# A layer-norm, causal-attention and expert-FFN layer on one core: the eight steps ahead of the attention written out, with the first batch's stacks read back during them

## The reference

```
xn   = (x - mean(x)) / sqrt(var(x) + 1e-5)                    # per row
# attention branch: 16 heads of 8 channels
Q, K, V = relu(xn @ Wq + bq), relu(xn @ Wk + bk), relu(xn @ Wv + bv)
scores  = Q K^T / sqrt(8); NEG where the key's row sums to 0; NEG above the diagonal
attn    = softmax(scores), set to 0 where the query's row sums to 0
s       = gamma * norm(attn V + xn) + beta
# FFN branch
x_attn  = norm2(xn) @ attn_w.T + attn_b + xn
eo      = gelu(x_attn @ w1[e] + b1[e]) @ w2[e] + b2[e]        # expert e fixed by position
f       = gelu(eo @ next_w.T + next_b)
out     = x + s * silu(f)
```

## Time and profile before

| | |
|---|---|
| median of 3 runs | 537.47 us (536.09 to 538.89) |
| profiled execution, its own time | 538.71 us |
| span of the profile, first to last instruction | 536.9 us |
| PE busy | 447.4 us (83%) |
| DVE busy | 406.4 us (76%) |
| ACT busy | 315.3 us (59%) |
| POOL busy | 124.7 us (23%) |
| mean granted TensorE clock | 0.942 |
| DMA packets, bytes | 28585, 39.68 MB |

### The profile page before, as it was taken

The page is one execution under the profiler, slowest core; times in us unless marked ns, Lnnn a source line. Parts: engine busy times, 40 slices in busy tenths (PEclk is TensorE's granted clock), DMA queues, the critical chain, the costliest instruction groups (busy, mean ns, idle before and its releaser), DMA issues.

```text
span 536.9 us, 10757 instructions
## 1 busy us (share of the span) xinstructions
PE 447.4 (83%) x3773; PEld 275.3 (51%) x3773; DVE 406.4 (76%) x1008; ACT 315.3 (59%) x670; POOL 124.7 (23%) x345
## 2 busy tenths in 40 slices
PE   0049545988999739999999999999999999999981
PEld 0026334766777515565555555555556556556540
DVE  6898988887884238576977877877878878887715
ACT  0029135977888803566656666656667567566670
POOL 8000000000000011001045045045054063072181
PEclk9999958989999955799999999999999999999997
DMA  8900021223333351122122222322212213212000
GB/s 220 295 20 0 20 80 43 75 80 98 98 98 88 110 146 22 47 76 62 56 83 67 72 67 66 85 56 66 85 53 77 82 46 93 64 48 69 2 21 20
DMA packets 28585, 39.68 MB, mean 74 GB/s; under 512 B 5751, under 2 KB 19959, under 8 KB 28535
## 3 DMA queue, kind: packets, MB, share of 16 engines
q1 hardware_dynamic: 28486, 39.03, 26.0%
q10 hardware_dynamic: 48, 0.01, 0.0%
HBM read 25.91 MB, written 10.49 MB: 68 GB/s over the span
## 4 chain that ended last, share of the span: by engine, by line
PE 55%; DVE 6%; issue 1%; ACT 1%; DVEq 0%; ACTq 0%
PE banks L979 15%; PE banks L1010 14%; PE banks L998 13%; PE banks L981 6%; PE banks L1000 5%; DVE mx L837 3%; PE banks L1020 3%; DVE stats L879 1%; DVE aggr L883 1%; ACT pt L950 0%; ACT ots L934 0%; PE banks L988 0%; DVE res L866 0%; DVE res L869 0%; DVE mixed L870 0%
## 5 line engine op out<-in xcount | busy, mean ns | idle before, releaser
L837 DVE TENSOR_REDUCE mx<-banks 128x1 f32<-128x384 f32 (+3 forms) x384 | 212.5, 598 | 59.7 <-PE banks L981 52.5
L950 ACT ACTIVATE pt<-banks 128x512 f32<-128x512 f32 (+2 forms) x384 | 184.8, 528 | 110.4 <-PE banks L1000 104.1
L981 PE MATMUL banks<-causal,ident_b 128*128 128x128 bf16 x512 | 106.8, 228 | 0.0
L1000 PE MATMUL banks<-causalT,ident_b 128*128 128x128 bf16 x512 | 103.7, 222 | 0.0
L979 PE MATMUL banks<-w_room 73*128 73x512 bf16 (+3 forms) x256 | 75.3, 331 | 11.5 <-DVEq L912 10.3
L1010 PE MATMUL banks<-pt,vg 128*9 128x512 f32 (+3 forms) x1024 | 81.9, 438 | 0.5 <-ACT pt L950 0.5
L998 PE MATMUL banks<-w_room 76*128 76x512 bf16 (+3 forms) x256 | 71.2, 310 | 0.0
L979 PE MATMUL banks<-k_odd,q_odd 73*128 73x512 bf16 (+3 forms) x256 | 69.0, 302 | 1.6 <-DVE mx L837 1.6
L998 PE MATMUL banks<-q_odd,k_odd 76*128 76x512 bf16 (+3 forms) x256 | 67.6, 300 | 2.0 <-ACT pt L950 2.0
L750 POOL TENSOR_SCALAR mneg<-mx 128x16 f32<-128x16 f32 x32 | 8.1, 253 | 197.9 <-DVEq L845 197.9
L981 PEld LDWEIGHTS banks<-causal,ident_b 128*128 128x128 bf16 x512 | 52.1, 102 | 0.0
(11 more groups left out here) (155 smaller groups left out, 615.7 us busy)
## 6 DMA issues: line engine op xcount, KB each, us to landing
k_scratch<-parts SPq DMA_DIRECT2D x40, 128.0 KB, 2.3
w_room<-q_scratch SPq DMA_DIRECT2D x48, 96.0 KB
w_room<-k_scratch SPq DMA_DIRECT2D x48, 96.0 KB
q_odd<-q_scratch SPq DMA_DIRECT2D x48, 96.0 KB
k_odd<-k_scratch SPq DMA_DIRECT2D x48, 96.0 KB
q_scratch<-parts SPq DMA_DIRECT2D x24, 128.0 KB, 2.3
w_room<-in_w_dram SPq DMA_DIRECT2D x1, 2048.0 KB, 9.2
xn_all<-xn_st SPq DMA_DIRECT2D x8, 256.0 KB, 2.4
```

Of the source, the lines that this page charges most:

```text
L837: ins = dve.tensor_reduce(mx[:, u % 2, heads[0]:heads[-1] + 1, q], banks[:, S0 + c % RING, 0:w * len(heads)].rearrange("p (h k) -> p h k", ...
L950: act.activation(weights(k, heads[0], len(heads)), banks[:, ST0 + j % RING, 0:(T - P * k) * len(heads)], ACT.Exp, scale=SCALE).then_inc(ex ...
L981: ins = mm(o[:, w - P:w], ident_b[:, :], causal[:, :], start=False, stop=True)
L1000: ins = mm(o[:, 0:P], ident_b[:, :], causalT[:, :], start=False, stop=True)
```

## The change

1. The hardware loops of SP, ACT and PE in the first block are gone. Their eight steps are written out.
2. The buffers `cen` and `work` of the first block are now the memory of `xn_all` and `gate_all`. `quotients` writes the normalised rows straight into `xn_all`, in place. The staging buffer `xn_st`, its DMA on SP and the semaphores `keep_ready`, `xn_kept`, `norm_free` and `w1_done` are gone.
3. Batch 0's stacks have a pair of their own (`q_own`, `k_own`), and the weights' rooms serve the odd batches. SP issues the ones after step 1's stores, and the query and key stacks of groups 0 to 3 after the stores of steps 2 to 5 (6 DMAs each). The second block's loads of groups 2 and 3 and of the odd ones ahead of its loop are gone.
4. The mask is made in the last step: DVE computes `live_all` and `mask_b` before `gate` and `lows`, PE transposes between the two expert products, ACT copies it in the place of the second norm. The store to `mask_scratch` is now on SP's queue after the last K stores. SP waits for it, reads the four mask rows, then reads the odd ones, and then waits for the last Q and K stores.
5. The last step no longer makes the second norm, the transposes and the attention-weight product of a step that doesn't exist.

```diff
-    qx, kx = [stack_of(w1_room)], [stack_of(w2_room)]
+    q_own, k_own = sb("q_own", [P, E * HID]), sb("k_own", [P, E * HID])
+    qx, kx = [stack_of(q_own), stack_of(w1_room)], [stack_of(k_own), stack_of(w2_room)]
...
-        cen = s1("cen", [P, NT, C])
-        work = s1("work", [P, NT, C])
+        cen, work = xn_all, gate_all
...
             def _(sp):
...
-                with sp.Fori(0, MB) as m:
-                    tok = Tokens(sp)
-                    for n in range(STEPS):
-                        sp.wait_ge(keep_ready, tok.next(keep_ready))
-                        sp.dma_start(xn_all[:, bass.ds(m * MT + TB * n, TB), :], xn_st[:, n]).then_inc(xn_kept[n], 16)
-                        for o in range(2):
-                            sp.wait_ge(low_ready, tok.next(low_ready))
-                            for k in range(COPIES[o]):
-                                dst = (q_dram, k_dram)[o][bass.ds(m * STEPS + n, 1), k].rearrange("b d h t -> (b h) d t")
-                                sp.dma_start(dst, parts[:, o, k % PARTS, :]).then_inc(parts_out[o], 16)
-                    tok.settle()
-
-
-                sp.wait_ge(w1_done, MB * STEPS)
-                load_queries(sp, 0, 0, 0)
-                load_queries(sp, 0, 0, 1)
-                sp.wait_ge(w2_done, MB * STEPS)
-                load_keys(sp, 0, 0, 0)
-                load_ones(sp, 0)
-                load_keys(sp, 0, 0, 1)
+                tok = Tokens(sp)
+                for i in range(B):
+                    for o in range(2):
+                        sp.wait_ge(low_ready, tok.next(low_ready))
+                        for k in range(COPIES[o]):
+                            dst = (q_dram, k_dram)[o][i:i + 1, k].rearrange("b d h t -> (b h) d t")
+                            sp.dma_start(dst, parts[:, o, k % PARTS, :]).then_inc(parts_out[o], 16)
+                    if i == 1:
+                        load_ones(sp, 0)
+                    if 2 <= i < 2 + NG:
+                        load_queries(sp, 0, 0, i - 2)
+                        load_keys(sp, 0, 0, i - 2)
+                sp.wait_ge(maskT_ready, 1)
+                sp.dma_start(mask_dram, maskT[:, :]).then_inc(mask_out, 16)
                 sp.wait_ge(mask_out, 16)
-                load_mask(sp, 0, 0, 0)
-                load_mask(sp, 0, 0, 1)
+                for g in range(NG):
+                    load_mask(sp, 0, 0, g)
+                sp.wait_ge(w2_done, B)
+                load_ones(sp, 1)
+                for o in range(2):
+                    sp.wait_ge(parts_out[o], 16 * COPIES[o] * (B + 1))
...
-                def quotients(m, n):
-
-                    tiles = slice(m * MT + TB * n, m * MT + TB * n + TB)
+                def quotients(i):
+
+                    tiles = slice(TB * i, TB * i + TB)
...
-                    if m > 0:
-
-                        dve.wait_ge(norm_free, n + 1)
-                        dve.wait_ge(xn_kept[n], 16)
...
-                            (wu, nr, quo, ALU.add, xn_st[:, n])):
+                            (wu, nr, quo, ALU.add, xn_all[:, tiles, :])):
...
                     dve.sem_inc(xn_ready, 1)
-                    dve.sem_inc(keep_ready, 1)
...
-                for i in range(2, MB * STEPS):
-                    quotients(i // STEPS, i % STEPS)
+                for i in range(2, B):
+                    quotients(i)
                     rests(tok)
                     if i == 2:
                         second_roots(GROUPS[1])
-                    sums(i // STEPS, i % STEPS)
+                    sums(i)
+                    if i == B - 1:
+                        link(dve.tensor_scalar(live_all[:, :], zero_all[:, :], -1.0, 1.0, ALU.mult, ALU.add))
+                        dve.tensor_scalar(mask_b[:, :], zero_all[:, :], -BIG, None, ALU.mult).then_inc(mask_ready, 1)
                     gate(tok, i - 2)
                     lows(tok)
...
-                def gelu_out(tok):
+                def gelu_out(tok, last):
...
-                    product_out(tok)
+                    if not last:
+                        product_out(tok)
...
-                with act.Fori(0, MB) as m:
...
-                        second_norm(tok, (n + 1) % STEPS)
...
+                for i in range(B):
...
+                    if last:
+                        act.wait_ge(maskT_done, 1)
+                        act.activation(maskT[:, :], banks[:, TRX, :].bitcast(BF16)[0:NT, 0:P],
+                                       ACT.Copy).then_inc(maskT_ready, 1)
+                    else:
+                        second_norm(tok, i + 1)
...
-                act.wait_ge(maskT_ready, 1)
-                act.dma_start(mask_dram, maskT[:, :]).then_inc(mask_out, 16)
...
+                    if i == B - 1:
+                        pe.wait_ge(mask_ready, 1)
+                        pe.transpose(banks[:, TRX, :].bitcast(BF16)[0:NT, 0:P], mask_b[:, :],
+                                     ident_b[:, :]).then_inc(maskT_done, 1)
...
+                    if i < B - 1:
+                        second_normed(tok, i + 1)
+                        normed(tok, i + 1)
+                    next_product()
+                    if i < B - 1:
+                        attn_product(tok, i + 1)
...
-                for o in range(2):
-                    sp.wait_ge(parts_out[o], 16 * COPIES[o])
-                for g in range(2, NG):
-                    load(0, 0, g)
-                load_ones(sp, 1)
                 tok = Tokens(sp)
                 maxima(tok, 0, 0)
```

More of the change, by code:

```diff
@@ L211, in build_program @@
         xn_ready, sums_ready = sem("xn_ready"), sem("sums_ready")
-        xl_ready, xn_kept = sem("xl_ready"), [sem(f"xn_kept{n}") for n in range(STEPS)]
-        keep_ready = sem("keep_ready")
-        norm_free = sem("norm_free")
+        xl_ready = sem("xl_ready")
         trx_done, trl_done = sem("trx_done"), sem("trl_done")
@@ L542, in _ @@
[L542 to L546 removed]
+                for i in range(B):
+                    n, last = i % STEPS, i == B - 1
+                    for o, bias, done in ((0, bq, q_done), (1, bk, k_done)):
+                        act.wait_ge(done, tok.next(done))
+                        act.wait_ge(parts_out[o], tok.next(parts_out[o], 16 * COPIES[o]))
+                        act.activation(full[:, o, :], banks[:, QB + o, :], ACT.Relu, bias=bias)
+                        act.activation(parts[:, o, 0, :], banks[:, QB + o, :], ACT.Relu,
+                                       bias=bias).then_inc(split_ready, 1)
+                    act.wait_ge(v_done, tok.next(v_done))
+                    at = slice(TB * i, TB * i + TB)
+                    act.activation(v_all[:, at, :].rearrange("p n (h w) -> p n h w", w=VW)[:, :, :, 0:DH],
+                                   banks[:, VB, :].rearrange("p (n h d) -> p n h d", n=TB, d=DH),
+                                   ACT.Relu).then_inc(vb_free, 1)
+                    for h in range(2):
+                        bank = H0B if h == 0 else QB
+                        for j in range(HC):
+                            if j % 2 == 0:
+                                act.wait_ge(h_done, tok.next(h_done))
+                            ins = act.activation(hid[:, h, j, :],
+                                                 banks[:, bank + j // 2, EC * (j % 2):EC * (j % 2) + EC],
+                                                 ACT.Gelu, bias=b1[2 * n + h][j])
+                        ins.then_inc(hid_ready, 1)
+                        act.wait_ge(rest_ready, tok.next(rest_ready))
+                        act.activation(parts[:, h, 1, :], rest[:, h, :], ACT.Copy).then_inc(mid_ready, 1)
+                    if last:
[4 more added lines that the diff above has]
+                        second_norm(tok, i + 1)
+                    act.wait_ge(eo_done, tok.next(eo_done))
+                    for h in range(2):
+                        ins = act.activation(eoT[:, EC * h:EC * h + EC], banks[:, XB, EC * h:EC * h + EC],
+                                             ACT.Identity, bias=b2[2 * n + h])
+                    ins.then_inc(eoT_ready, 1)
+                    if not last:
+                        second_out(tok)
+                        norm_out(tok, i + 1)
+                    gelu_out(tok, last)
@@ L552, in _, with normed, second_normed @@
                 pe.wait_ge(consts, 2)
-                def transposes(tok, n, ready, rows_u, bank, done):
-                    pe.wait_ge(ready, tok.next(ready))
+                def normed(tok, i):
+                    pe.wait_ge(xn_ready, tok.next(xn_ready))
                     for k in range(TB):
-                        ins = pe.transpose(banks[:, bank, P * k:P * k + P], rows_u[:, n, k, :], ident[:, :])
-                    ins.then_inc(done, 1)
-                def normed(tok, n):
-                    transposes(tok, n, xn_ready, xn_st, TRX, trx_done)
-                def second_normed(tok, n):
-                    transposes(tok, n, xl_ready, xl_st, TRL, trl_done)
```

(20 more changed lines are left out.)

165 lines of the change are left out of this document (50 added, 115 removed).

## The result

The changed kernel took 530.18 us, the median of 4 runs (528.99 to 531.01), against 537.12 us of the kernel before beside it. The profiled execution took 530.05 us, its span is 528.2.

The account below looks back on a forecast made before the run. It took DVE to pace the first block's steps, SP's DMA issue to bound the passage, and PE the attention. Steps 2.7 plus tail 1.95, say 4.7 us, gave 532.8 us, 8-in-10 range 530.3 to 536.6.

Parts of the forecast that it names:

- The regimes and the chain: Whole kernel: attention PE-bound and untouched; gain from first block, paced by DVE, and passage, bound by SP's DMA issue.
- SP's tail: Passage after the last K stores: SP's remaining DMAs and waits take 7.4 us instead of 9.35, 1.95 less.
- its stated bounds: Mask store's landing in SP's tail: taken as 3.2 us, bounded between 2.3 and 3.7.
- Earlier writes ahead of an increment: Mask store behind 5 K stores: by the skill page's rule, up to 0.4 us more landing time.
- Table loads and DVE's waits: First block, step 4: ACT's load and DVE's waits go; 2.2 us earlier, then 2.9; bounds 1.5 to 3.7.
- Increments: DVE in the first block's eight steps: one fewer per step, 0.1 us each, 0.8 at most.
- The written-out store: First block's loops: 0.27 us of ACT loop end goes at step 4; no price for shorter SP issue.
- The early loads cost nothing: SP's stack and ones loads during the steps: priced at nothing, at most about 2 us over three steps.
- Rival 2, about 531: More than the sum: 0.7 from the wait at 114.50, up to 1.5 from PE's clock and drain; chance 0.14.
- the drain beside a table load: ACT in the first block: skill page's drain of about 1.38 us, worth 1.4 more; given chance 0.02.
- Rival 3, the clock: Attention stays longer at the lower clock: 3.6 us lost per unit, slower from 1.3 units; chance 0.10.
- its sign of 3 us: Start of the attention: a clock rising more than 3 us later against PE's start would show the slower-clock case.

Follow-up runs that it names:

- e4: Changed kernel with batch 0's stacks and ones loaded where they were before, after the last K stores and in the second block; 533.66 us, ratio 0.9931.
- e7: Changed kernel with the mask store issued by ACT right behind its copy instead of by SP; 528.57 us, ratio 0.9853 against the kernel before.
- e2: Kernel before with only ACT's loop written out; 535.54 us, ratio 0.9974.
- e3: Kernel before with only SP's loop written out; 534.09 us, ratio 0.9936.
- e5: Kernel before, unchanged, profiled once more in a single execution; 536.12 us, span 534.3.
- e9: Kernel before with only PE's loop written out; 537.84 us, ratio 1.0017.
- e8: e7 with the mask rows of groups 2 and 3 and the odd ones also moved into the second block; 525.90 us, ratio 0.98.
- e6: Changed kernel with five more increments of an unused semaphore on DVE in each of the eight steps; 533.70 us.
- e12: e8 with DVE releasing the score banks before its preparations and 3 unused fp32 products behind PE's last product of the first block; 526.52 us.
- e1: Changed kernel run again, unchanged, as the mark for the others; 529.91 us, ratio 0.9858.
- e13: e8 with DVE releasing the score banks before its preparations and an unused 128x512 fp32 product after every third lead chunk; 522.79 us, ratio 0.9726.
- e14: As e13, but with unused products of 128x256; 521.18 us, ratio 0.9717 against the kernel before.

## Why the prediction was wrong, step by step

- **The regimes and the chain: right.** The gain is in the steps and the passage, and the attention kept its length from its first product on, within 0.5 us. e4 splits the change: 3.2 us for the steps (533.66 against 536.85), 3.75 for the passage.
- **SP's tail: the failed step.** The prediction put it at 7.4 us, 1.95 less than before, and said "The store took 3.2 us to land from ACT's queue". It measured 5.91, 3.46 less. 1.3 of the 1.5 us that were missing is the mask's landing, 1.9 us against 3.2, outside its stated bounds too: they came from stores of 128 KB, and the mask has 8 KB. The other 0.2 is a shorter issue of the ones and a shorter gap ahead of the mask store. It is not the queue: in e7 the same store from ACT's queue also took 1.9. In the five traces in which SP was issuing stack loads around it (before, e2, e3, e5, e9) it took 3.0 to 3.8, with loads only behind it (e4) 2.2, with none 1.7 to 1.9. Before the change nobody waited for it, so its row had no price on the chain; the change took the stack loads away from around it and made it the wait. The Trainium skill's page "DMA: Bandwidth & Descriptors" (Latency and other measured facts) says that a lighter load of HBM makes the fixed cost of a DMA smaller. The runs agree with it only in part: with the loads gone the store landed sooner, but in e7, with the DMA engines as busy with stores of 128 KB (0.75, 203 GB/s), it also took 1.9. What it is about the stack loads that costs 1.3 us stays open.
- **Earlier writes ahead of an increment: no effect seen.** The mask's store took 1.9 us to land behind 5 K stores, as it did from ACT's queue between the Q and the K stores (e7, e8). The Trainium skill's page "DMA: Bandwidth & Descriptors" (Queues, rings and completion order) lets an increment land only after the earlier writes of its DMA engine; of the 0.4 that this might have added the trace shows nothing, so those writes had landed by then or did not count.
- **Table loads and DVE's waits: right in kind, read from a disturbed stretch.** 2.2 us at step 4 was counted from waits of which 1.67 was the clock's fall in that execution (e5). Against e5, SP's first Q store of step 4 comes 2.0 us earlier (132.66 against 134.68), that of step 5 2.8 (147.37 against 150.21). That is near the forecast 2.2 and 2.9, partly by luck: the shorter bursts of stores, which the prediction priced at nothing, are in it.
- **Increments: right.** 0.095 us each against 0.1 (e6).
- **The written-out store: not seen.** The prediction gave the loops' end on ACT a price and SP's shorter issue none. It is 0.58 us for the last step alone, more where K's landing is waited for (e3), and it took the 0.79 at 114 with it, which the prediction had left standing.
- **The longer code's own price: not seen.** 0.5 to 0.9 us in a burst in e9, up to 1.0 in the changed kernel (4.23 against e3's 3.19), so the steps gained 3.1 and not the 4.1 that e2 and e3 add up to, with the increments on top; part of that is also that e2 and e3 take away the same waits.
- **The early loads cost nothing: right,** as far as two traces of one kernel agree (e4).
- **Rival 2, about 531**, came nearest to the result, and partly for its reason: the 0.79 at 114 did go. But PE's clock in step 3 was an accident of one execution, not something that the change takes away. For the drain beside a table load, which the Trainium skill's page "ScalarE: Activation LUTs" (What ACT_TABLE_LOAD costs) states, nothing spoke: e2, with the loads of step 4 gone, gained 1.3 us in all.
- **Rival 3, the clock: did not come.** The rise was 26.4 us after the start against 25.8, far from its sign of 3 us. That it set "the same idle stretch" against the risk was no argument: the stretch went from 10.31 to 7.65 us without effect, and in e12 the clock fell after hardly any.

The errors in the steps nearly cancelled, which is luck: 2.7 forecast, 3.08 measured against e5 (183.06 to 179.98), or 2.24 with e1's trace (180.82). The tail gave 3.46 or, with e1, 3.40. By profiles, from e5 to the changed kernel's first, the whole is 6.1: 3.08 and 3.46, less 0.45 in the attention (339.9 in e5, 340.4 after). The medians differ by 6.9, because that of the kernel before stands 1.0 above e5's time and that of the changed kernel 0.1 above its profiled time; where these 0.9 come from no trace shows. So of the 2.3 us by which the gain was larger than forecast, the tail is 1.5, shown in two traces; the other 0.8 lies in the steps, the attention and the medians, and its cause is open.

## What to carry to other kernels

When a change makes someone wait for a transfer that nobody waited for before, its old landing time belongs to what was being issued around it then: bound it from both sides, with transfers of its own size, and ask what the change takes away from there. Before summing waits of one profile, look for a stretch in it that another execution may not have, here a fall of PE's clock; one more profile of the same kernel would have shown it. The same holds for judging an experiment: e12's trace lost 1.6 us to such a fall ahead of the edit. And a serial tail on one queue is best emptied of all that the next stage's first work does not need.

## What the hardware showed that I had not expected

- A DMA with its address written out is issued faster: 8 stores in 5.08 us against 5.66 in a loop.
- A 16 KB block on the instruction queue and an SP burst that takes 0.5 to 1.0 us longer came together in the traces of e9 and of the changed kernel; which of the two makes the other is not shown, only that they came with PE's longer code.
- An 8 KB store landed in 1.9 us amid stores of 128 KB, with the DMA engines 0.75 busy (e7), and in 3.0 to 3.8 us amid stack loads, with them about as busy.
- In e12 PE's clock fell 5.0 us after a start at the full level, and in the changed kernel it stayed at 0.50 for 26.4 us in which PE was busy nearly throughout. With one dense fp32 product of no use after every third chunk it came back 6.5 (e13) and 10.0 us (e14) after the start. What it is about those products that brings it back (their type, their length, the weight loads between them) the runs don't tell apart.
